# Cross attention of layer 0 in a decoder kernel, its TensorE steps grouped by tile form

## The reference

```python
q = split_heads(hidden_states @ Wq, q_len)          # hidden_states = layernorm(x)
k = split_heads(hidden_states @ Wk, q_len)
v = split_heads(hidden_states @ Wv, q_len)
q, k = rope(q), rope(k)
scores = jnp.einsum('bhqd,bhkd->bhqk', q, k) * inv_sqrt_d + attention_mask
scores = jnp.maximum(scores, jnp.finfo(scores.dtype).min)
w = softmax(scores)
attn_output = jnp.einsum('bhqk,bhkd->bhqd', w, v)
a_k = split_heads(adapter @ Wk, adapter_len)        # adapter: 8 x 375 x 512
a_v = split_heads(adapter @ Wv, adapter_len)
a_scores = jnp.tanh(gate) * softmax(jnp.einsum('bhqd,bhkd->bhqk', q, a_k) * inv_sqrt_d)
attn_output = attn_output + jnp.einsum('bhqk,bhkd->bhqd', a_scores, a_v)
return attn_output @ Wo                             # added to x
```

## Time and profile before

| what | us |
|---|---|
| median of 3 runs | 2147.83 |
| lowest and highest | 2144.65, 2153.28 |
| the profiled execution | 2144.4 |
| its span, first to last instruction | 2142.6 |
| of it, before the cross attention's first scores | 453.3 |
| cross attention (453.3 to 1098.0) | 644.7 |
| behind it | 1044.6 |

### The profile page before, as it was taken

One profiled execution on the slowest core, in us unless ns is written; L12 is line 12 of the kernel. 1 busy time (PEld: TensorE's weight loads), 2 busy tenths in 40 slices (PEclk: granted clock), 3 DMA queues, 4 the chain that ended last, 5 costly groups with the idle time before them and its releaser, 6 DMA issues.

```text
span 2142.6 us, 29151 instructions
## 1 busy us (share of the span) xinstructions
PE 1929.8 (90%) x11802; PEld 1222.0 (57%) x11802; DVE 1040.7 (49%) x1920; ACT 577.5 (27%) x1867; POOL 392.1 (18%) x456
## 2 busy tenths in 40 slices
PE   6799999989999999999883999948999999989898
PEld 5575665545565565665563777737657754444344
DVE  3564555435656655655632111116454453544599
ACT  0322223214444444444520010101222130212411
POOL 3332322311011010110002000023111100000378
PEclk9899999999999999999866999978999999999999
DMA  9000002000000000000124787760000034432010
GB/s 370 1 1 1 1 1 93 1 22 15 2 15 16 1 15 16 1 16 1 60 119 138 291 317 290 288 243 18 1 1 1 15 120 189 180 145 112 0 35 35
DMA packets 30821, 170.70 MB, mean 80 GB/s; under 512 B 3832, under 2 KB 3832, under 8 KB 17024
## 3 DMA queue, kind: packets, MB, share of 16 engines
q1 hardware_dynamic: 28128, 161.50, 19.8%
q0 software_dynamic: 2560, 7.34, 1.2%
HBM read 155.98 MB, written 16.52 MB: 81 GB/s over the span
## 4 chain that ended last, share of the span: by engine, by line
PE 71%; DVE 13%; issue 5%; ACT 4%; DMA 4%; POOL 3%; SPq 0%; POOLq 0%; DVEq 0%; ACTq 0%
PE PS L1100 7%; PE PS L888 5%; PE PS L937 5%; PE PS L1180 5%; PE PS L1140 5%; PE PS L977 4%; PE PS L1210 3%; PE PS L1109 3%; PE PS L968 3%; PE PS L1016 2%; DMA R<-in_ctx 2%; PE PS L945 2%; PE PS L1000 2%; ACT R L1848 2%; PE PS L1036 2%
## 5 line engine op out<-in xcount | busy, mean ns | idle before, releaser
L1979 POOL TENSOR_TENSOR rstd<-veps,mhalf 112x1 f32<-112x1 f32 (+1 forms) x76 | 57.7, 759 | 732.5 <-DVE veps L1270 718.2
L1100 PE MATMUL PS<-R,W 128*128 128x128 f32 x1344 | 156.5, 278 | 17.6 <-issue 17.6
L1848 ACT ACTIVATE R<-PS,nmx 112x375 f32<-112x375 f32 x256 | 144.4, 574 | 96.8 <-DVE nmx L1396 96.8
L1100 PEld LDWEIGHTS PS<-R,W 128*128 128x128 f32 x1344 | 153.1, 193 | 22.2 <-issue 22.2
L1799 ACT ACTIVATE R<-PS,small 112x112 f32<-112x112 f32 x256 | 87.0, 378 | 228.0 <-DVE small L1309 228.0
L1016 PE MATMUL PS<-cst,R 112*125 112x112 f32 x768 | 135.8, 301 | 4.1 <-ACT rT L1872 3.8
L1396 DVE TENSOR_REDUCE nmx<-PS 112x2 f32<-112x750 f32 x128 | 114.4, 931 | 47.1 <-PE PS L1000 47.0
L1016 PEld LDWEIGHTS PS<-cst,R 112*125 112x125 f32 x768 | 102.6, 194 | 49.9 <-issue 37.2
L888 PE MATMUL PS<-xT,W 128*128 128x224 f32 x640 | 127.0, 356 | 0.0
L1341 DVE TENSOR_TENSOR x<-x,PS 112x512 f32<-112x512 f32 x40 | 27.5, 688 | 202.2 <-PE PS L1180 90.8
L888 PEld LDWEIGHTS PS<-xT,W 128*128 128x128 f32 x640 | 121.3, 192 | 5.8 <-issue 5.3
(11 more groups left out here) (274 smaller groups left out, 3340.3 us busy)
## 6 DMA issues: line engine op xcount, KB each, us to landing
W<-in_we SPq DMA_DIRECT2D x63, 1024.0 KB, 6.7
W<-in_entwT SPq DMA_DIRECT2D x8, 1024.0 KB, 4.9
W<-in_entpw SPq DMA_DIRECT2D x8, 1024.0 KB, 7.5
W<-in_ctxT SPq DMA_DIRECT2D x8, 750.0 KB, 4.3
R<-in_ctxT SPq DMA_DIRECT2D x8, 750.0 KB
R<-in_ctx SPq DMA_DIRECT2D x8, 750.0 KB
xs_rows<-in_x SPq DMA_DIRECT2D x3, 1792.0 KB, 38.8
R<-xs_rows SPq DMA_DIRECT2D x21, 256.0 KB, 6.7
```

Source lines behind the costliest of these rows:

```text
L1100: o = e.matmul(PS[:, m, c * 128:(c + 1) * 128], gate_up(j % 3, k, off + c * 128), BT[:, j % 2, k, :], start=k == 0, stop=k == 3)
L1848: e.activation(p_of(b, c, par)[0:S, r, :], PS[0:S, r, 0:SC], ACT.Exp, bias=nmx[0:S, par, r:r + 1], accum_out=sums[0:S, b % 2, n:n + 1]).th ...
```

## The change

- `attendx` returns for each gap a head and a tail. The head holds the pieces of the task's softmax and all turns of task n - 2 (one each in turn), then the exponentials as steps of their own: `xe` (own) or two `ce` (context), which only ACT takes part in. The tail holds the row sums and all value steps of task n - 3, with `xu` behind the odd context task. `cross` puts the fill of a gap between head and tail instead of spreading it.
- On ACT the exponentials so come behind the copies of the turns in the same gap; before, each stood at its maximum.
- `xd` moves one task later. `xd` and `xr` go to the tail, `xb` and `xw` to the head.
- `GAP` of own tasks is 3.0 instead of 2.0, which moves fill into gaps of own tasks.
- `turned_by`: of the three turns of a context task the first two are copied by ACT, the third by DVE (before: in turn over six).
- The ring of probabilities has six buffers instead of four. The two new ones lie in `row`, over biases that the first attention has read.

```diff
-GAP = {"own": 2.0, 0: 5.5, 1: 5.5}
+GAP = {"own": 3.0, 0: 5.5, 1: 5.5}
...
-    gaps, lag = [], []
-    for n in range(len(TASKS) + 2):
-        out, pieces = [], shifts(n)
-        if n < len(TASKS) and TASKS[n][2] != "own":
-            out, pieces = pieces[:1], pieces[1:]
-        if n >= 2:
+    gaps = []
+    for n in range(len(TASKS) + 3):
+        turns, tail, mine = [], [], shifts(n)
+        if 2 <= n < len(TASKS) + 2:
             b, c, kind = TASKS[n - 2]
             turns = [("xt", b, c, par) for par in range(2)] if kind == "own" else [("xct", b, c, kind, t) for t in range(3)]
-            for t in turns:
-                out += [t] + pieces[:1]
-                pieces = pieces[1:]
-                lag.append(("xv" if t[0] == "xt" else "xcv", *t[1:]))
-                if len(lag) > 3:
-                    out.append(lag.pop(0))
...
+        head = []
+        for k in range(3):
+            head += mine[k:k + 1] + turns[k:k + 1]
+        if n < len(TASKS):
+            b, c, kind = TASKS[n]
+            head += [("xe", b, c)] if kind == "own" else [("ce", b, c, kind, r) for r in (0, 2)]
+        if 2 <= n < len(TASKS) + 2 and TASKS[n - 2][2] == "own":
+            tail.append(("xm", *TASKS[n - 2][:2], 3))
+        if n >= 3:
+            b, c, kind = TASKS[n - 3]
+            tail += [("xv", b, c, par) for par in range(2)] if kind == "own" else [("xcv", b, c, kind, t) for t in range(3)]
+            if kind == 1:
+                tail.append(("xu", b, c))
+        gaps.append((head, tail))
     for b in range(NBATCH):
-        for k, step in ((1, ("xd", b)), (3, ("xr", b)), (4, ("xb", b)), (5, ("xw", b))):
+        for k, step in ((2, ("xd", b)), (3, ("xr", b)), (4, ("xb", b)), (5, ("xw", b))):
...
-            out += spread(gaps[n], some, cost) if gaps[n] else some
+            out += head + some + tail
...
-    return (par if k == "xt" else 1 + par * 3 + step[4]) % 2
+    return par if k == "xt" else int(step[4] == 2)
...
-        PX = [carve(448) for _ in range(3)] + [X1[:, 7644:8092]]
+        PX = [carve(448) for _ in range(3)] + [X1[:, 7644:8092], row[:, 0:448], row[:, 448:896]]
...
-        px_of = {s: PX[n % 4] for n, s in enumerate(pxs)}
+        px_of = {s: PX[n % 6] for n, s in enumerate(pxs)}
```

More of the change, by code:

```diff
@@ new lines, in attendx @@
+        if 2 <= n < len(TASKS) + 2 and TASKS[n - 2][2] == "own":
[6 more added lines that the diff above has]
+        gaps.append((head, tail))
+    for b in range(NBATCH):
+        for k, step in ((2, ("xd", b)), (3, ("xr", b)), (4, ("xb", b)), (5, ("xw", b))):
+            head, tail = gaps[min(12 * (b + 1) + k, len(gaps) - 1)]
+            if step[0] in ("xd", "xr") or 12 * (b + 1) + k >= len(gaps):
+                tail.append(step)
+            else:
+                head.append(step)
@@ L281, in attendx @@
             if step[0] == "xw":
-                out.append(("stats", 2, b))
+                tail.append(("stats", 2, b))
     return gaps
@@ L299, in cross @@
         mine = range(12 * b, 12 * b + 12)
-        whole = sum(cost(s) for s in fill + late) + sum(cost(s) for n in mine for s in gaps[n])
+        whole = sum(cost(s) for s in fill + late) + sum(cost(s) for n in mine for part in gaps[n] for s in part)
         unit = whole / sum(GAP[TASKS[n][2]] for n in mine)
@@ L307, in cross @@
             due += unit * GAP[TASKS[n][2]]
-            rest = [(s, 0) for s in gaps[n]]
-            due -= sum(cost(s) for s in gaps[n])
+            head, tail = gaps[n]
+            due -= sum(cost(s) for s in head + tail)
             some = []
@@ L313, in cross @@
                 some.append(fill.pop(0))
-            out += spread(gaps[n], some, cost) if gaps[n] else some
-    for g in gaps[len(TASKS):]:
-        out += g
+            out += head + some + tail
+    for head, tail in gaps[len(TASKS):]:
+        out += head + tail
     return out
@@ L1835, in cv, with xe, ce @@
                                  ACT.Copy).then_inc(*up("even_out", ("cv", b, t)))
-            def xm(b, c, piece):
-                if piece == 2:
-                    w.wait_ge(*at("shifted", (b, c)))
-                    e.activation(SX[0:S, c % 2, :], SX[0:S, c % 2, :], ACT.Exp).then_inc(*up("sexp", (b, c)))
-            def cm(b, c, par, first):
+            def xe(b, c):
+                w.wait_ge(*at("shifted", (b, c)))
+                e.activation(SX[0:S, c % 2, :], SX[0:S, c % 2, :], ACT.Exp).then_inc(*up("sexp", (b, c)))
+            def ce(b, c, par, first):
                 if b >= 2:
@@ L1964, in wave @@
                 sines(H[:, t, :], s_, c_, float(np.pi), ("w", t))
[L1966 to L1967 removed]
+            do = {"turn": turn, "turnh": turnh, "m0": m0, "v0": v0, "pj": pj, "vx": vx, "ck": ck, "cv": cv, "xe": xe,
+                  "ce": ce, "xt": xt, "xct": xct, "xu": xu, "xr": xr, "route": route, "gu": gu, "dn": dn, "td": td, "c1": c1, "p1": p1,
                   "v1": v1, "r5": r5, "t5": t5, "wc": wc, "eb": eb, "sine": sine, "bound": bound, "wave": wave}
```

8 lines of the change are left out of this document (removed).

## The result

| | before | after |
|---|---|---|
| median of four runs, us | 2149.84 | 2085.38 |
| lowest and highest | 2144.65, 2153.28 | 2084.55, 2086.40 |
| span of the profiled execution | 2142.6 | 2082.7 |
| cross attention, first xs to last xr | 453.3 to 1097.8 | 453.9 to 1036.5 |
| behind it | 1044.8 | 1046.2 |

The ratio is 0.9702, with a 95% interval of 0.9680 to 0.9724: 64 us faster by the medians, where a gain of 39 was forecast. The time lies only 1.4 us inside the low end of the range (2084), less than two executions of one kernel can differ. The gain is in the cross attention: the stage is 61.9 us shorter between the two profiled executions, which are 59.9 us apart; what stands behind the stage takes 1.4 us longer and starts earlier as a whole, as forecast.

The account below looks back on a forecast made before the run. PE's work was taken to bound the cross attention; 53 us gained from fewer form changes less 14 us of new waits, all else 0, gave -39 us: 2105.4 against the profiled 2144.4, about 2107 as median, range 2084 to 2141.

Parts of the forecast that it names:

- rival A: PSUM banks empty in time or the clock gains: the whole 53 us remains, 2094, or 2082 with the clock; chance 0.20.
- Form changes: PE in cross attention: 630 changes of tile form become 300, at 0.18 or 0.14 us each; gain 53 us, bounds 46 to 66.
- Rival D: The price per form change is not real and reappears as matmul time inside runs; 2148 to 2155 us, chance 0.06.
- New waits: PE waits for PSUM bank copies in own tasks without fill, some old waits replaced; net cost 14 us, bounds 0 and 28.
- rival B: PSUM evictions become the bound: waits double to 28 us and heavy places spread; gain 17 us, 2131 us, chance 0.14.
- Exponentials behind the copies: On ACT: next scores wait for exponentials, hidden except in batch 7, which gains about 8 us already counted; taken as 0.
- Copies: 32 context turn copies move from DVE to ACT: ACT +17 us, DVE -20 us, neither becoming the bound; no separate gain.
- Rings: Six probability buffers remove a copy's wait for an older value step; no PE row shows one, so 0 us.
- Own share: Share 3.0 puts fill into 13 own tasks instead of one, sparing them the new waits; 0 beyond the counts.
- Clock: Half-clock time in the cross attention, costing about 35 us: no reason for a sign, taken 0, 12 us either side.
- Rival C: Slower: clock drops in grouped stretches; 87 us more at half clock cancels the gain, 2194 at worst; chance 0.08.

Follow-up runs that it names:

- mixed: The changed kernel with a value step behind each turn again, not grouped; 2118.9 us, ratio 0.987 to the kernel before.
- split: The changed kernel with one value step of each gap's tail put ahead of the fill; 2102.6 us, ratio 0.98 to the kernel before.
- mixed_early: The changed kernel with a value step behind each turn again and the exponentials directly behind their maxima; 2177.9 us, ratio 1.0135 to the kernel before.
- early_exp: The changed kernel with the exponentials put back directly behind their maxima; 2175.7 us, ratio 1.0149 to the kernel before.
- own_late: The changed kernel with the own exponential behind the next context task's exponentials and the third own-side turn copied by ACT; 2055.1 us, ratio 0.9567 to the kernel before.
- act3: The changed kernel with the third turn behind own scores copied by ACT instead of DVE; 2090.1 us, ratio 0.974 to the kernel before.
- gap2: The changed kernel with the old fill share of own tasks, 2.0 instead of 3.0; 2090.6 us, ratio 0.9743 to the kernel before.

## Why the prediction was right, and where its steps were not

The sign, the place (the stage alone), and the two mechanisms of its sum were right. The size was not: it missed by 22 us, and that the time still falls into the range, by 1.4 us, is luck; the low end came from rival A. The measured time is one that A gives (2082 to 2094). The half of A that has the clock gain did happen; the half by which the banks empty in time did not. A slip of 2 us stands in the sum itself: 2105.4 and 3.4 are 2108.8, not 2107.

1. *Form changes, forecast -53.* By work in the table -46 between the kernels; mixed and split give 0.126 and 0.139 us per change, where the mean price taken was 0.16. The prices of a step inside and at the end of a run are in the rows as they were; the sum over the stage comes out 7 us lower, at the low bound (46). Kernels with the same order differ by more than that in work, and at 0.32 us for a us at the low level the term would be 50, so the shortfall is not told from the roughness of the measure. Rival D is out. The Trainium skill (TensorEngine Tiling, Key Properties) says that changing the tiling mode drains the TensorE. The runs here show a price of 0.13 to 0.14 us per change of form, which fits that; the draining itself they don't show.
2. *New waits, forecast +14 net.* The grouped order alone costs 11.2 us of idle time (mixed to after), so the mechanism and nearly the size were right: 12.1 us for the third copy, 1.9 for the mask addition (L1006 for DVE L1380) and 4.0 for copies by ACT (L1866, in small waits of up to 0.3), 18.0 in all where 18.4 were worked out, the third copy in just the 15 places counted and two of batch 7. By place the sizes were otherwise: most places have 0.3 us for the third copy and 0.2 for ACT's, and the dearest single wait, 1.25 us, is in three places that the step held to be ordinary. Net it was -2.1, because 13.3 us of old waits went with the rest of the change (before to mixed), where the step let only 4 go. This is the first mis-sized term: 16 us. Rival A, by which the banks empty in time, is not what happened; nor are rival B's 28 us.
3. *Exponentials behind the copies, taken 0.* This term was put at nothing, and the runs show that it is large. The chain was worked out rightly, for batch 7 too: from xs to second xc 8.5 us were forecast in place of 10.1, and the timeline after shows 977.45 - 968.97:

```profile
968.97 0.66 PE L995 MATMUL PS<-R 32*112 32x112 f32 x16
...
977.45 1.20 PE L1006 MATMUL PS<-W,R 32*112 32x375 f32 x8 [2.22 <-ACT R L1853]
```

   But the step asked only whether the later exponentials would delay the next scores, not what they give the copies ahead of them, nor what gathering the fill does. With gathered fill, late exponentials are worth 59 us in mixed order and 90 in grouped order; with spread fill they would cost 119.
4. *Copies, taken 0:* 26 us in the grouped order. 5. *Rings, 0:* not tried apart. 6. *Own share, 0 beyond the counts:* 4.6 us of idle time, unclear in time.
7. *Clock, taken 0 with 12 to either side.* It was -13.8: 30.7 us less at the low level. This is the second mis-sized term, and part 7 says itself that it had no reason for a sign. That the low level comes with waits, several runs show. mixed_early against mixed, and early_exp against after, have 28 and 60 us more idle time and 57 and 65 us more at 1.2 GHz; own_late has 12.5 and 31 less. For the change itself this is no answer, since its idle time is only 2.1 us less than before and its time at the low level 30.7 less; where that gain of the clock comes from stays open. Rival C had the mechanism and needed 87 us more at the low level than the kernel before has; the changed kernel has less, and early_exp, where the waits are, has 34 more.

The sum of the measured terms is -46 - 2 - 14 = -62, the 61.9 us of the stage. It closes by the way "work" is defined, and is no test of the three terms. Of the 23 us beyond the forecast's -39, 16 are the waits, 14 the clock, and -7 the form changes.

## What to carry to other kernels

Where an engine that reads PSUM also does other work, ask of each piece of that work what stands behind it in its list, and change its place together with the order of what fills the time: each of two edits alone lost here what both together gained. A wait with two releasers close behind each other (DVE's copy and ACT's) goes only when both are moved, so one failed repair says little against the other. Grouping matmuls of one tile form was worth 0.13 to 0.14 us per change of form avoided; another 10 to 14 us (estimates from the clock record) came with the clock, for a reason not shown.

## What the runs showed of the hardware

Idle time of PE of about a microsecond can be paid again by the clock. 18 us from the own scores of batch 1, block 1, in the changed kernel, where PE waits 1.25 us at 545.5; the last number but two is the granted clock:

```profile
541.00:559.00 18.00, 16.60 (x135) 10.90 (x128) 9.96 (x15) 6.17 (x16) 0.00 (x0) 0.81 0.00 1
```

and the 18 us from the same own scores in own_late, where it doesn't wait so and gets further, 177 matmuls for 135:

```profile
535.70:553.70 18.00, 17.71 (x177) 10.92 (x174) 12.02 (x18) 9.79 (x27) 0.00 (x0) 1.00 0.01 1
```

The level falls to 1.2 GHz behind the wait, and the spreading matmuls take 3.72 us instead of 2.00. The changed kernel has this wait of 1.25 us in three places (they end at 546.7, 699.1 and 778.6), and each time a stretch of 6.8 us at 1.2 GHz begins within 2.4 us (547.9, 701.5, 780.0); own_late has no such wait in batches 1 to 6 and runs them wholly at the full clock. It does not follow from each wait, though: behind the wait of 1.03 us of the same kind in the next block (569.7, 722.3, 801.6) the clock stays each time. The length alone does not decide it either: act3 has three waits of 1.50 us (544.3, 696.6, 776.0), each with a fall (544.2, 697.8, 776.3), and three of 1.48 us one block later (569.0, 720.0, 800.8) with none. And gap2 has 4.6 us more idle time than the changed kernel and as much time at 1.2 GHz. Over the stage the two move together only roughly (the table), and single runs of one kernel differ by up to 16 us (gap2).

Twelve float transposes in one go (541.64 above) take 1.49 us from start to start inside this stretch, all of it at the full clock, which was granted before they began:

```profile
541.00:545.00 4.00, 4.00 (x64) 2.84 (x57) 3.90 (x6) 1.34 (x3) 0.00 (x0) 1.00 0.00 0
```

The Trainium skill (TensorE: Matmul & The Clock Gate, PE-mode transpose) says that the fast clock does not engage for transposes in transpose mode. These rows show that twelve in one go do not end it. Whether transposes alone would bring it on no run here shows, nor does the trace tell whether these are of that mode.
